# A fused four-layer transformer kernel: token statistics by the vector engine's batch-norm instructions, two stages fewer, places by TensorE

## The reference, cut to what matters

```python
xn = _layernorm(x)                                   # layer 0: first norm
x_norm = xn * rsqrt(mean(xn * xn) + 1e-6) * w        # RMS norm of the same token, for layer 0's attention
# layer 2, attention: banded over the 17 last positions
attn_out = softmax(scores) @ k_win
x1 = _layernorm(x + attn_out, g1, be1)
kn = kv / max(norm(kv), 1e-12)                       # unit keys of all tokens and of 10 slots P
kp = kn @ Wi.T + bi; hdd = silu(kp @ Wl1.T + bl1); hdd = silu(hdd @ Wl2.T + bl2)
pred = hdd @ mem_W.T + mem_b; grad_W = 2/(n*m) * (pred - kp).T @ hdd
# layer 2, ffn: each of 8 experts takes its 512 best tokens
scores, token_idx = top_k(softmax(x @ gate).T, k=512)
```

## Time and profile before

| | |
|---|---|
| three runs | 2136.36, 2128.51, 2137.08 us; median 2136.36 |
| the profiled execution | 2138.4 us, of which the span (first to last instruction) is 2136.6 us |
| busy over the span | PE 85%, DVE 63%, ACT 48%, POOL 18% |
| mean granted TensorE clock | 0.827 |

### The profile page before, as it was taken

How to read it: one execution, slowest core, us unless ns; L and a number is a source line. 1 busy time by engine, 2 the same in 40 slices (tenths; PEclk the granted TensorE clock), 3 DMA queues, 4 the chain that set the end, 5 groups by cost and what they waited for, 6 DMA issues and landing times.

```text
span 2136.6 us, 33764 instructions
## 1 busy us (share of the span) xinstructions
PE 1807.6 (85%) x11206; PEld 1218.2 (57%) x11206; DVE 1340.5 (63%) x5024; ACT 1026.4 (48%) x2474; POOL 383.6 (18%) x511
## 2 busy tenths in 40 slices
PE   6889578777777779898999888989899854999998
PEld 5465466666666646666577766545544542973333
DVE  3687888888888854587554676342211331559996
ACT  2433465566666633454543224544443223437787
POOL 0000100000000000141452002003144023506652
PEclk9999666666666757998999558989999967998999
DMA  2000200000000000000001400011023100624662
GB/s 117 1 13 13 52 20 20 26 20 20 20 20 20 14 35 1 1 2 7 0 1 38 124 1 1 1 50 28 15 20 60 79 17 32 120 69 85 111 115 39
DMA packets 95469, 76.26 MB, mean 36 GB/s; under 512 B 22336, under 2 KB 87232, under 8 KB 94528
## 3 DMA queue, kind: packets, MB, share of 16 engines
q1 hardware_dynamic: 87616, 65.57, 13.0%
q0 software_dynamic: 7680, 8.53, 2.2%
HBM read 49.12 MB, written 23.51 MB: 34 GB/s over the span
## 4 chain that ended last, share of the span: by engine, by line
PE 55%; DVE 29%; ACT 7%; issue 4%; another core or an unknown queue 1%; SPq 1%; DMA 1%; DVEq 0%; POOL 0%; PEld 0%; PEldq 0%; ACTq 0%; POOLq 0%
PE ps L212 51%; DVE sm L233 9%; DVE big L239 5%; ACT big L221 4%; DVE mw L233 3%; DVE big L225 2%; PE ps L216 2%; PE ps L2603 2%; DVE big L233 1%; DVE tmp L229 1%; ACT sm L221 1%; SPq L873 1%; DVE sm L229 1%; DVE ke L225 1%
## 5 line engine op out<-in xcount | busy, mean ns | idle before, releaser
L221 ACT ACTIVATE tmp<-ps,bi 128x512 f32<-128x512 f32 (+1 forms) x226 | 153.9, 683 | 211.6 <-PE ps L212 205.8
L212 PE MATMUL ps<-big,mw 128*128 128x512 f32 (+3 forms) x476 | 231.3, 593 | 14.9 <-DVEq L260 7.2
L221 ACT ACTIVATE sm<-sm 128x1 f32<-128x1 f32 x512 | 174.0, 340 | 106.6 <-DVE sm L233 96.0
L221 ACT ACTIVATE big<-ps,co 128x512 f32<-128x512 f32 (+1 forms) x296 | 173.9, 649 | 44.1 <-PE ps L212 39.8
L212 PE MATMUL ps<-big,co 128*128 128x256 f32 (+1 forms) x344 | 170.1, 629 | 25.3 <-DMA bi<-bia 11.6
L225 POOL TENSOR_TENSOR big<-big,co 128x512 f32<-128x512 f32 x32 | 40.1, 1275 | 724.2 <-ACT big L220 670.9
L239 DVE TENSOR_REDUCE big<-ps 128x2 f32<-128x512 f32 x256 | 159.2, 670 | 6.8 <-PE ps L212 6.7
L212 PE MATMUL ps<-big,tmp 128*32 128x256 f32 (+2 forms) x1180 | 130.5, 404 | 24.9 <-DVE tmp L229 19.5
L212 PE MATMUL ps<-ke 48*128 48x256 bf16 (+4 forms) x638 | 125.2, 309 | 30.7 <-DVE big L225 16.7
L212 PEld LDWEIGHTS ps<-big,mw 128*128 128x128 f32 (+1 forms) x476 | 93.3, 230 | 79.8 <-issue 47.4
L212 PE MATMUL ps<-ke,big 128*128 128x32 f32 (+1 forms) x608 | 84.2, 286 | 64.0 <-ACT big L220 64.0
(11 more groups left out here) (264 smaller groups left out, 3893.5 us busy)
## 6 DMA issues: line engine op xcount, KB each, us to landing
mw<-d_tab SPq DMA_DIRECT2D x32, 328.0 KB, 3.5
mw<-m SPq DMA_DIRECT2D x2, 4096.0 KB, 13.1
d_pt<-big SPq DMA_DIRECT2D x32, 192.0 KB
ke<-d_pt SPq DMA_DIRECT2D x72, 64.0 KB
big<-d_pt SPq DMA_DIRECT2D x72, 64.0 KB
mw<-d_pt SPq DMA_DIRECT2D x48, 64.0 KB
d_xs<-big SPq DMA_DIRECT2D x1, 2560.0 KB, 9.3
big<-d_xs SPq DMA_DIRECT2D x5, 512.0 KB, 6.5
```

Of the source, the lines that this page charges most:

```text
L212: return e.matmul(out, lhsT, rhs, start=start, stop=stop)
L221: return e.activation(out, in_, f, bias=K("zero")[0:out.shape[0], :] if bias is None else bias, scale=scale, **kw)
```

## The change

- **first_norm** works token-major: a second copy of x (`xK`) is loaded to `big4`, DVE takes mean and variance of each block by bn_stats and bn_aggr, ACT makes both roots, DVE one reciprocal a tile; DVE writes the layer norm by one two-scalar operation a block, POOL writes 28 of the 32 blocks of the RMS norm (DVE the other 4), PE transposes both, and ACT copies them out. The stage begins with the identity matrix and the first quarter of `xK`; all other constants come later, and so does `xT`.
- **dense** also writes the unit keys token-major (`KNT3`), from the same statistics: four small operations and four of 128x128 a tile on DVE, one more root on ACT.
- **choose** also makes the ten slot keys.
- **window** leaves its weights undivided; one operation on DVE scales the weighted sum by 1/sum and adds the residual, now token-major, and bn_stats and bn_aggr follow for each block. PE turns the unit keys feature-major, four blocks every fourth step, and ACT copies them. DVE waits at the start for the write of `d_acc`, whose source `big0` it overwrites.
- **lna** and **keys** are gone, with two barriers.
- **memory** begins with the places, by eleven matmuls and accumulations on PE; it contains `digits_dve`, `hot_dve`, `list_pe` and the end of the list, which were in keys; two PSUM banks less are left for its own matmuls, so that two of its four matmuls of a tile have one bank each. POOL normalises the 32 blocks of x1 (`unit_pool`).
- **grad** also transposes x1 (PE) and copies it with gain and bias (ACT).

```diff
         def first_norm_dve(e, dn):
...
             for s in range(NT + 1):
                 if s < NT:
...
+                    for k in range(4):
+                        e.bn_stats(n0_stat[:, s % 2, k, :], XK3[:, 4 * s + k, :]).then_inc(dv, 1); n_s = dn.up()
+                        if k:
+                            e.wait_ge(dv, n_s - (1 if k == 1 else 2))
+                            e.bn_aggr(n0_agg[:, s, k - 1, :], n0_stat[:, s % 2, k - 1, :]).then_inc(dv, 1); dn.up()
...
+                    e.reciprocal(rst2(t), rst2(t)).then_inc(n0_rcp.sem, 1)
...
+                    for k in range(4):
+                        ts(e, XH3[0][:, 4 * t + k, :], XK3[:, 4 * t + k, :], n0_agg[:, t, k, 0:1], rst2(t)[:, k:k + 1], SU, MU).then_inc(n0_a.sem, 1)
+                    if t % 2 == 0:
+                        ts(e, XH3[1][:, 4 * t + 3, :], XK3[:, 4 * t + 3, :], n0_agg[:, t, 3, 0:1], rst2(t)[:, 7:8], SU, MU).then_inc(n0_c.sem, 1)
...
+        def first_norm_pool(e):
+            for t in range(NT):
+                e.wait_ge(*n0_rcp(t + 1))
+                for k in range(4 if t % 2 else 3):
+                    ts(e, XH3[1][:, 4 * t + k, :], XK3[:, 4 * t + k, :], n0_agg[:, t, k, 0:1], rst2(t)[:, 4 + k:5 + k], SU, MU).then_inc(n0_b.sem, 1)
...
         def win_dve(e, dn):
+            triangle_dve(e)
+            e.wait_ge(s_z, 16)
...
-                    ts(e, sc_, sc_, wz[:, k:k + 1], None, MU).then_inc(wn_p.sem, 1)
...
-                    tt(e, X1[:, q0:q0 + 128], PS[:, 3 + k % 3, 256:384], XN[:, q0:q0 + 128], AD).then_inc(wn_x.sem, 1)
+                    e.wait_ge(*wn_rz(k + 1))
+                    stt(e, X1T3[:, k, :], PS[:, 3 + k % 3, 256:384], wz[:, k:k + 1], XT3[:, k, :], MU, AD).then_inc(wn_x.sem, 1)
+                    if k:
+                        win_aggr_dve(e, k - 1)
+                    e.wait_ge(*wn_x(k + 1))
+                    e.bn_stats(LNST[:, k % 2, :], X1T3[:, k, :]).then_inc(wn_st.sem, 1)
...
         def win_pe(e):
...
-                    e.wait_ge(*wn_p(k + 1))
+                    e.wait_ge(*wn_exp(k + 1))
...
+                    quad(e, PS[:, 7, :], lambda j: KNT3[:, 4 * g + j, :]).then_inc(wn_kq.sem, 1)
...
+        def places_pe(e):
...
+            mm(e, PS[:, 7, :], K("lt"), SE, stop=False)
+            e.wait_ge(*tk_sc(1))
+            e.wait_ge(*tk_tri(1))
+            for k in range(4):
+                p = mm(e, PS[:, 7, 128 * k:128 * k + 128], TOT[:, k:k + 1].broadcast_to((128, 128)), TRI8, start=False, stop=(k == 3))
+                if k < 3:
+                    mm(e, PS[:, 7, 128 * k + 128:512], *below(k, 3 - k), start=False, stop=False)
...
+        def mem_dve(e, dn):
+            listed(e)
+            digits_dve(e, dn)
+            e.wait_ge(*me_sd(1))
+            e.reciprocal(LNR, LNR).then_inc(me_rcp.sem, 1)
             for u in range(NT + 1):
+                if u < NT:
+                    hot_dve(e, dn, u)
+                if u:
+                    mem_diff_dve(e, u - 1)
...
+        def unit_pool(e):
+            e.wait_ge(*me_rcp(1))
+            for k in range(32):
+                ts(e, X1T3[:, k, :], X1T3[:, k, :], LNAG[:, k, 0:1], LNR[:, k:k + 1], SU, MU).then_inc(un_x.sem, 1)
...
+        def unit_act(e, g):
+            e.wait_ge(*gr_u(g + 1))
+            act(e, X1[:, sl(g)], PS[:, 5 + g % 2, :], ACT.Identity, scale=B("g21"), bias=B("be21")).then_inc(gr_uc.sem, 1)
```

More of the change, by code:

```diff
@@ L105 @@
 STAGES = """first_norm kqv first scan read ln1 norm1 lengths retention norm2 ffn1 dense choose
-    window lna keys memory grad gate lnb ffn2 lnc experts shared ln3 turned top1 qkv energy e3""".split()
+    window memory grad gate lnb ffn2 lnc experts shared ln3 turned top1 qkv energy e3""".split()
 def after(name):
@@ L358, in first_norm_pe @@
         def first_norm_pe(e):
+            e.wait_ge(s_id, 16)
+            for t in range(NT):
+                for w in range(2):
+                    if t > 1:
+                        e.wait_ge(*n0_cp(2 * (t - 2) + w + 1))
+                    for k in range(4):
+                        if w == 0:
+                            e.wait_ge(*n0_a(4 * t + k + 1))
+                        elif t % 2 == 0 and k == 3:
+                            e.wait_ge(*n0_c(t // 2 + 1))
+                        else:
+                            e.wait_ge(*n0_b(pool_blocks(t, k)))
+                        p = tr(e, PS[:, 2 * w + t % 2, 128 * k:128 * k + 128], XH3[w][:, 4 * t + k, :])
+                    p.then_inc(n0_turn.sem, 1)
+                if t == 3:
+                    e.wait_ge(s_c, 16)
+                    e.wait_ge(*tq_sum(2))
+                    mm(e, PS[:, 6, 0:2], K("one"), qs[:, 0:2]).then_inc(tq_ps.sem, 1)
@@ L374, in first_norm_pe @@
[L374 to L385, removed]
@@ L1756, in program @@
         IDX = small(32).bitcast(mybir.dt.uint32).rearrange("p (h l) -> p h l", h=2)
-        LST = [SCN[:, 512 + 256 * i:768 + 256 * i] for i in range(2)]
-        EYE8 = SCN[0:8, 1152:1280]
         def prefix_pe(e, i, m):
@@ L1774, in prefix_dve @@
             tt(e, out, x, PS[:, 0, 0:256], AD).then_inc(dv, 1); e.wait_ge(dv, dn.up())
+        pk = small(50)
+        pkn, pkp, ph1, ph2, pdf = (pk[:, 10 * i:10 * i + 10] for i in range(5))
+        pk_sq, pk_len = signals("scalar", 1, 1)
+        pk_cols, pk_bc = signals("tensor", 1, 1)
+        pk_rcp, = signals("vector", 2)
         def topk_pe(e):
+            e.wait_ge(*pk_sq(1))
+            mm(e, PS[0:10, 7, 0:1], TMP[:, 8, 0:10], K("one", 0, 1)).then_inc(pk_cols.sem, 1)
             logits_pe(e, W("gw2"), 8)
@@ new lines, in sums_of_blocks_pe, with sums_of_blocks_act, below @@
+            p.then_inc(tk_sum.sem, 1)
+        def sums_of_blocks_act(e):
+            e.wait_ge(*tk_sum(1))
+            act(e, TOT, PS[:, 6, 0:4], ACT.Copy).then_inc(tk_sc.sem, 1)
+        def places_pe(e):
+            def below(k, n):
+                return TOT[:, k:k + 1].broadcast_to((128, 128)), BLK8.rearrange("p (r n) -> p r n", r=1).broadcast_to((128, n, 128))
+            mm(e, PS[:, 7, :], K("lt"), SE, stop=False)
+            e.wait_ge(*tk_sc(1))
+            e.wait_ge(*tk_tri(1))
+            for k in range(4):
+                p = mm(e, PS[:, 7, 128 * k:128 * k + 128], TOT[:, k:k + 1].broadcast_to((128, 128)), TRI8, start=False, stop=(k == 3))
+                if k < 3:
+                    mm(e, PS[:, 7, 128 * k + 128:512], *below(k, 3 - k), start=False, stop=False)
+            p.then_inc(tk_pl.sem, 1)
@@ L3173, in _ @@
             de_pool(e, gn)
-            e.wait_ge(stage_end, after("window"))
-            places_pool(e, gn)
+            unit_pool(e)
             e.wait_ge(stage_end, after("lnb"))
```

400 lines of the change are left out of this document (185 added, 215 removed).

## The result

Four runs of the changed kernel took 2062.8 to 2068.9 us, median 2067.6; four of the kernel before beside them 2128.5 to 2143.0, median 2136.7. The ratio is 0.9685, with a 95% interval of 0.9659 to 0.9712: 3.15% faster, where 2081 us (2.6%) was forecast. The profiled execution took 2068.9 us, span 2067.0.

A forecast was written before the change was run, and what follows sets the result against it. Bounds were read by stage: lna and keys chains, memory PE's, window DVE's. From 2138.4 us, -69.3 - 9.0 + 1.1 + 0.7 - 7 + 23 + 5.2 = -55.3 gave 2083, rounded to 2081 us; range 2062 to 2104.

The forecast's parts named there:

- the likeliest case: First norm and memory: DVE's and POOL's operations alternate, each waiting for the other's end; 2083 us in all, chance 55%.
- the second rival: DVE's runs stay together and POOL slips into its pauses; 2065 us, or 2062 with the window's full 9 us; chance 22%.
- POOL beside DVE: First norm and memory: one engine's operation waits for the other's end, adding 9.6 us to the first norm.
- First norm: Opening stage: 51.1 us falls to 32.5 undisturbed, or to 42.1 with POOL and DVE alternating, a gain of 9.0.
- undisturbed sum: Whole kernel without any disturbance by POOL: stage changes add up to -72.9 us, giving 2065.5 us.
- Memory: Memory stage: 45 us undisturbed, 15 more than before; 53 us, +23, with POOL's operations alternating with DVE's on each table.
- Window: Window stage: DVE's 0.59 us wait for PE's count can go, 9 us at most; 7 us taken as gained.
- the bound "0": Window: if PE, given four more transposes every fourth step, became the bound, the net gain would be 0.
- Grad: Grad stage: ACT's, gets eight copies of 128x512 at 0.65 us each, +5.2 us; PE's transposes lie beside them.
- Choose: Choose stage: waits for the slot keys' square and a ten-row matmul ahead of its gate matmuls, +0.7 us.
- What would show it: Expected marks by stage, among them first norm ending at 40 to 44 us and DVE's 128x128 writes averaging above 0.35 us.
- the three signs of being wrong: POOL's operation outside 0.42 to 0.85 us, memory's PE falling to half clock, or window steps staying at 2.7 us.

## Why the prediction came out as it did

The direction and the range were right, and the likeliest case was not: 2083 us were to come from DVE and POOL alternating. The number is the second rival's, at 22%: its sum, 2065.5 us, is 2 us off. Its mechanism is so only in part: POOL did not slip into DVE's pauses, it ran without one from 8.39 to 32.23 us, and neither engine held the other for the length of an operation.

- **POOL beside DVE** is the step that failed. It took a wait behind a POOL operation with two tensors for the law of any pair of operations. The new POOL operation has one tensor and two scalars, and beside it DVE's four writes took 1.17 us, not 2.3. The run with additions shows that the form of POOL's operation decides: there they alternate. That it is not POOL's time for one operation, the trace of the kernel before shows. In the same stretch as rows 7 DVE's same operation once started inside a long POOL operation with one tensor:

```profile
1293.03 1.51 POOL L229 TENSOR_SCALAR big<-big 128x512 f32<-128x512 f32 x1
...
1293.35 0.31 DVE L229 TENSOR_SCALAR sm<-sm 128x4 f32<-128x4 f32 x1 [1.10 <-ACT sm L221]
```

It took 0.31 us and ended 0.9 us before POOL's. Behind POOL's two-tensor operations it ended within 0.03 us of POOL's end, all three times (1.25 us at 1289.56 and 0.52 at 1296.21, beside rows 7). It is a single meeting, but it could have been read before the forecast.

The Trainium skill ("SBUF — State Buffer", Who interferes with whom) has an exclusive lock: who issues first holds the shared ports for the whole instruction. It counts DVE's `tensor_scalar`, the form of these writes, among the operations that can take them. The alternation in the run with additions fits that. Two measurements differ from it, and they decide. DVE's writes inside POOL's 0.85 us operations did not wait for their end. And in memory, by the starts on record, POOL's operation of 2.70 us began 0.38 us before DVE's first long one, yet POOL's was held, through two of DVE's, and DVE's were not. By the same section of the Trainium skill, DVE instructions with at most one SBUF input, outside the modes that use both ports, leave POOL alone; the 0.79 us beside statistics fits.

- **First norm**, forecast -9.0, undisturbed -18.6, measured -17.5 and -18.4. The terms of the undisturbed sum add up to 32.6 us, and the stage took 33.6. The start was 4.9 us, not 4.3, and ACT's load of its table (1.28 us at 6.26) was not in the sum. POOL's price was put at 0.5 us and is 0.79 alone, 0.85 here; for this reason POOL ends the stage, some 2 us behind DVE.
- **Memory**, forecast +23, undisturbed +15, measured +15.5 and +16.0. Places, reciprocal and list came within 0.5 us of their times. Even with alternation little would have been lost: with POOL's additions memory took 45.9 us, since PE's 4.3 us a tile (list matmuls at 1288.02 and 1292.33) cover DVE's tables. The forecast had counted that cover once (4 us), not for every tile.
- **Window**, forecast -7, measured -2.2 and -3.2. The wait was put down to the transposes waiting for DVE's product; they stopped waiting, but the count stands behind other matmuls at half clock, as the run with the count first shows. At that clock two steps take what they took before, so the bound "0" was right there; what was gained came with the full clock, which the forecast did not have.
- **Grad** +4.8 and +4.9 (forecast +5.2), though PE's rather than ACT's: ACT's copy of 128x512 took 0.77 us, not 0.65. **Dense** +1.2 (+1.1). **Choose** -0.5 (+0.7): its end ran at the full clock (0.54 on average, 0.50 before). Whether the slot keys' work is also hidden under the gate matmuls is open. **lna and keys** -69.3, as forecast. The write of `d_acc` held the window's first count by 0.2 us.
- **What would show it** had a bad mark: a mean of DVE's writes above 0.35 us. The view counts each operation with its overlap, so it says 0.366 us for a run of four in 1.17 us (and 0.340 for the undisturbed run of 1.11). The length of the run was the thing to watch. Of the three signs of being wrong at the prediction's end one was met, the window's steps stayed at 2.7 us (5.44 for two), and one nearly: POOL's operation, with a mean of 0.855 us in the first norm, stands at the edge of the 0.42 to 0.85 us given, and in memory went far over it when held. The third was not, memory's PE kept 0.95 of its clock.

That the total fits to 2 us is partly luck: the touched stages fell short of the undisturbed sum (-72.9) by 4 to 5 us, and the others gave 1.8 us in the first pair, where qkv's 22 us less stands against more in scan and in the last stage.

## What to carry to other kernels

Before a wait between DVE and POOL is priced, look at what the operations read: here POOL's one-tensor operation with two scalars made DVE's run of writes 5% longer (1.17 us, from 1.11), its two-tensor addition 43% (1.59), and DVE's long tensor-tensor operations stopped POOL for up to 1.9 us. Look at every meeting of the two in the trace, not at the first one that fits. A delay on an engine that has slack in every tile is hidden in every tile, not once. When a wait is to go, follow the matmul that is waited for through PE's queue: removing what one matmul waits for leaves those that stand ahead of it.

## What the runs showed of the hardware

- POOL's subtract-and-multiply with two scalars on 128x128 float32 takes 0.79 us alone; its addition of that size, with two tensor inputs, 0.37 us each in a run beside DVE. With one fixed scalar it takes 0.85 us for 128x256 and 1.51 for 128x512 (kernel before). So the form sets the price, and not only the number of elements.
- In the stage qkv ACT and DVE stand still for some 22 us beside POOL's scatter of tokens in all eight profiles from two chips (in the first profile of the kernel before the waits were of 6.3, 2.1 and 15.4 us on ACT, put down to another core or an unknown queue) and in none of the three from another. The cause is open.
- Between chips the kernel before differed by 1.7% (2131 to 2168 us), and the last stage by 24 us between profiles (228 to 252).
